# Down projections of the first MLP's chunks, taken in pairs as seven block products

## The chip, the cores and the metric

The kernel runs on one core of a Trainium2 chip. The metric is the device time in microseconds. It took 2169.54 us, the median of three runs (2168.88 to 2170.97).

## The reference, cut to what matters

Two layers. Each has attention, an MLP called cms, a second MLP called mod, a clip, and an adapter with a layer norm. Four batches of 512 tokens with 512 features; the hidden width of both MLPs is 2048, everything is float32.

```python
attn_out = softmax(q @ k.T * scale) @ v @ Wp + bp
cms_out  = gelu(attn_out @ cW1 + cb1) @ cW2 + cb2 + target_embed
modifier = gelu(concat([attn_out, cms_out]) @ mW1 + mb1) @ mW2 + mb2
x = clip(x + cms_out + modifier, 0, 1)       # then the adapter
```

The change touches only `gelu(...) @ cW2`, the down projection of cms.

## The kernel before

Two batches (b = 0, 1) are worked on together; two layers of two such groups give four rounds. Activations lie transposed, 128 features x 512 tokens a tile. Each float32 operand is split into a high part, written by ScalarE's `Copy` into float32r, and a low part, written by VectorE as value minus high part. A product is three matmuls a tile pair, hi*hi, hi*lo and lo*hi (`tile`, lines 610 to 619).

Both MLPs run over the hidden width in eight chunks of 256. A slot n (0 to 15 a round) computes the up projection of chunk n and the down projection of the chunk before it: slots 0 to 7 are cms, 8 to 15 mod. Up projections use Strassen-Winograd's scheme: the four block products over (feature half, batch) are replaced by seven, Q1 to Q7, of sums of blocks (A11, A12, S1, S2, A22, S3, S4 for the weights; B11, B21, T1, B22, T2, T3, T4 for the activations). GpSimd forms the weight sums (`sums`, line 542), and in mod the hidden sums (`hidden_sum`, line 557). In mod the down projection also has seven products, whose inner halves are the two 128-feature tiles of one chunk. In cms it is plain: `down(r, n, b)` (line 826) gives for each batch four banks of PSUM, two inner tiles each, 24 matmuls, 48 a chunk; `down_add` (line 1483) adds each bank to `pc`.

The order is written out by hand, an own program for each engine (`slot` for ScalarE at line 1180 and for VectorE at line 1570, `mlp` for TensorE at line 853), tied by counting semaphores. A chunk's weights go from memory to one of three staging buffers, are summed there, and are split into `ring`, in pieces: part 0 of A (four blocks, 1024 columns), part 1 (three blocks, 768 columns), D (a plain down piece, 1024 columns). `weight_stream` (line 148) lists the pieces; a load waits until the last piece of the buffer's former content is split (`STAGE_FREE`). The A pieces of cms chunks alternate between stages 0 and 1, D uses stage 2. Other names: `take` is ScalarE's copy of an up product out of bank 0 or 1 (`prod_done` is TensorE's signal, `snapped` its own); `combine` is VectorE's sum of an up product and that copy, into `raw`; `gelu` writes `raw`; `hidden_hi` and `hidden_lo` split it.

## Time and profile before

| | us |
|---|---|
| median of three runs | 2169.54 |
| profiled execution | 2169.18 |
| its span | 2167.5 |
| TensorE busy | 2107.3 (97%) |
| VectorE busy | 1548.4 (71%) |
| ScalarE busy | 1042.0 (48%) |
| GpSimd busy | 646.2 (30%) |

PE is TensorE's matmuls, PEld its weight loads, DVE VectorE, ACT ScalarE, POOL GpSimd, SPq the queue of SyncE, which issues the loads. The profiled execution's time is 1.68 us more than its span. The duration in a matmul's row is its length in the pipeline; the next one begins before it ends. Queries used: the page, busy time by stretch, instructions in order of time of each engine, groups by line and form, and the waits.

### The profile page before, as it was taken

Reading aid. Unit: us, or ns where it says so; the run is one execution under the profiler, and the core shown is the slowest. Engines: PE = TensorE matmul, PEld = TensorE weight load, DVE = VectorE, ACT = ScalarE, POOL = GpSimd, SP = SyncE. Lnnn points to the kernel's source line nnn. Section 1 sums busy time; section 2 is a strip of 40 time slices with the busy share of each in tenths; the row PEclk is TensorE's granted clock in tenths of the full one; section 3 lists DMA queues with packets and bytes.
Section 4 is the critical chain, followed back from the end, with each engine's and each line's share of the span. In section 5 each row is a group of like instructions: output and inputs, shape, how many; then the busy total and the mean of one; then the engine's idle time right before and its main releaser. Section 6 shows DMA issues by size and latency. Waiting matters only on the chain.

```text
span 2167.5 us, 24870 instructions
## 1 busy us (share of the span) xinstructions
PE 2107.3 (97%) x9256; PEld 1724.2 (80%) x9256; DVE 1548.4 (71%) x1923; ACT 1042.0 (48%) x1527; POOL 646.2 (30%) x644
## 2 busy tenths in 40 slices
PE   8999998999999998999999999899999999999997
PEld 6888886888878886888877888688887888778884
DVE  4366678776867668876776766977686865887776
ACT  5264445544446444544554544444454644354444
POOL 1001147453001116655000111854400011475420
PEclk9999999999999999999999999999999999999999
DMA  8101111112302111112312111121130311112111
...
DMA packets 124615, 138.02 MB, mean 64 GB/s; under 512 B 5824, under 2 KB 100032, under 8 KB 123600
## 3 DMA queue, kind: packets, MB, share of 16 engines
...
## 4 chain that ended last, share of the span: by engine, by line
PE 83%; DVE 11%; ACT 3%; issue 2%; DMA 2%; SPq 0%; ACTq 0%; DVEq 0%
PE bank L615 27%; PE bank L617 27%; PE bank L616 27%; DVE ring L1321 2%; DVE vc L1363 2%; DMA fold_staging<-fold_w 1%; DVE pc L1493 1%; ACT ring L955 1%; DVE lsum L1695 1%; DVE xa L1358 1%; ACT raw L1098 0%; PE bank L923 0%; DVE xs L1700 0%; DVE xs L1653 0%; DVE xs L1685 0%
## 5 line engine op out<-in xcount | busy, mean ns | idle before, releaser
L550 POOL TENSOR_TENSOR stage<-stage 128x256 f32<-128x256 f32 x120 | 112.6, 938 | 1120.4 <-DMA stage<-cms_w 903.5
L1321 DVE TENSOR_TENSOR ring<-stage,ring 128x1024 fp32r<-128x1024 f32 (+1 forms) x312 | 365.1, 1181 | 103.8 <-ACT ring L955 103.5
L615 PE MATMUL bank<-ph_hi,ring 128*128 128x512 f32 x1048 | 410.6, 392 | 5.3 <-issue 2.4
L617 PE MATMUL bank<-ph_hi,ring 128*128 128x512 f32 x1048 | 407.9, 389 | 0.0
L616 PE MATMUL bank<-ph_lo,ring 128*128 128x512 f32 x1048 | 407.9, 389 | 0.0
L615 PE MATMUL bank<-xa,ring 128*128 128x512 f32 x1016 | 396.2, 390 | 5.7 <-DVE ring L1321 2.8
L617 PE MATMUL bank<-xa,ring 128*128 128x512 f32 x1016 | 395.3, 389 | 0.0
L616 PE MATMUL bank<-xa,ring 128*128 128x512 f32 x1016 | 395.3, 389 | 0.0
L955 ACT ACTIVATE ring<-stage 128x1024 fp32r<-128x1024 f32 (+1 forms) x312 | 296.3, 970 | 111.3 <-PE bank L617 78.3
L615 PEld LDWEIGHTS bank<-ph_hi,ring 128*128 128x128 f32 x1048 | 196.7, 188 | 53.7 <-issue 7.2
L616 PEld LDWEIGHTS bank<-ph_lo,ring 128*128 128x128 f32 x1048 | 196.8, 188 | 40.8 <-issue 0.7
L617 PEld LDWEIGHTS bank<-ph_hi,ring 128*128 128x128 f32 x1048 | 196.7, 188 | 40.8
L615 PEld LDWEIGHTS bank<-xa,ring 128*128 128x128 f32 x1016 | 190.7, 188 | 48.4 <-DVE ring L1321 7.9
L1517 DVE TENSOR_TENSOR ph_lo<-raw,ph_hi 128x512 fp32r<-128x512 f32 x312 | 213.7, 707 | 17.4 <-ACT ph_hi L1103 17.3
L617 PEld LDWEIGHTS bank<-xa,ring 128*128 128x128 f32 x1016 | 190.7, 188 | 39.6
L616 PEld LDWEIGHTS bank<-xa,ring 128*128 128x128 f32 x1016 | 190.7, 188 | 39.6
L615 PE MATMUL bank<-vc,ring 128*128 128x512 f32 x512 | 201.0, 393 | 16.9 <-DVE vc L1363 10.7
L617 PE MATMUL bank<-vc,ring 128*128 128x512 f32 x512 | 199.4, 389 | 0.0
L616 PE MATMUL bank<-vc,ring 128*128 128x512 f32 x512 | 199.3, 389 | 0.0
L1493 DVE TENSOR_TENSOR pc<-bank,pc 128x512 f32<-128x512 f32 x224 | 152.2, 688 | 60.6 <-PE bank L617 60.3
L1103 ACT ACTIVATE ph_hi<-raw 128x512 fp32r<-128x512 f32 x144 | 88.0, 629 | 200.2 <-PE bank L617 198.5
L1504 DVE TENSOR_TENSOR raw<-bank,snap 128x512 f32<-128x512 f32 x112 | 77.1, 688 | 144.5 <-PE bank L617 140.3
...
## 6 DMA issues: line engine op xcount, KB each, us to landing
stage<-mod_w SPq DMA_DIRECT2D x128, 256.0 KB, 3.3
...
```

The source lines that it names most:

```text
L550: pool.tensor_tensor(part(S1), part(S2), part(A22), ALU.add).then_inc(sums_ready, 1)
L615: pe.matmul(dst, lh, rh, start=start and n == 0, stop=False, skip_group_check=not start)
L616: pe.matmul(dst, lh, rl, start=False, stop=False, skip_group_check=not start)
L617: done = pe.matmul(dst, ll, rh, start=False, stop=n == last, skip_group_check=not start)
L955: act.activation(ring_part(key, 0), staged(key), ACT.Copy).then_inc(w_hi, 1)
L1103: act.activation(ph_hi[:, tile, :], raw[:, tile, :], ACT.Copy).then_inc(h_hi, 1)
L1321: dve.tensor_tensor(ring_part(key, 1), staged(key), f32(ring_part(key, 0)), ALU.subtract).then_inc(w_lo, 1)
L1358: dve.tensor_tensor(xa[:, 8 + 4 * b + k:8 + 4 * b + k + 2, :], src[:, b, k:k + 2, :], f32(xa[:, 4 * b + k:4 * b + k + 2, :]), ALU.subtract ...
L1363: dve.tensor_tensor(block_lo(t, blk, j, n), src, f32(block_hi(t, blk, j, n)), ALU.subtract).then_inc(lo_sem, 1)
L1493: done = dve.tensor_tensor(acc, src, acc, ALU.add)
L1504: dve.tensor_tensor(raw[:, to, :], bank[BANK[q]][:, :], snap[:, 0, :], ALU.add).then_inc(combined, 1)
L1517: done = dve.tensor_tensor(ph_lo[:, at, :], src, f32(ph_hi[:, at, :]), ALU.subtract)
```

## The change

Chunks (0,1), (2,3) and (4,5) of cms form pairs i = 0, 1, 2. A pair's down projection is one product with an inner width of 512: its inner halves are the two chunks, its outer halves the two halves of the 512 features, its columns the two batches. It is computed as seven block products of 2 x 2 tile pairs, 12 matmuls each. Of pair i, Q1 and Q5 run in its odd slot 2i+1, Q3 and Q6 in the even slot after it, Q7, Q4 and Q2 in the odd slot after that. Chunks 6 and 7 stay plain, in slot 7. What comes with it:
- a piece E a pair, with blocks of 512 columns, in stages 1 and 2 together; it is loaded by four transfers, summed by four 512-wide GpSimd additions, and split in four parts (1024, 512, 1024, 1024 columns). All A pieces now use stage 0;
- GpSimd forms eight hidden sums a pair (T1, T3, T2, T4 for both tiles), and fourteen tiles a pair are split where eight were;
- a buffer `raw_odd` for the odd chunk's hidden tiles, and places in `vc` for high and low parts; both are free in cms;
- seven adds of 1024 columns a pair into `pc` where sixteen of 512 stood (the first ones with the bias stay 512 wide);
- up products start with Q5 in slots 2 to 7, Q3 comes ahead of Q7 in slots 1 to 6;
- slot 7: the remaining products of pair 2, then both plain down projections of chunk 6, then the rest; D of chunk 7 is split ahead of them.

```diff
+PAIR_AT = {A11: 0, S1: 1, A12: 2, A22: 3, S2: 4, S3: 5, S4: 6}
+PAIR_PARTS = ((0, 2), (6, 1), (2, 2), (4, 2))
+PAIR_RING_GROUP = (4, 11, 14, 4)
...
+def up_order(n):
+    return 0 if n == CH - 1 else 1 if n == SLOTS - 1 else 3 if 1 < n < CH else 2
...
     def staged_up(r, n):
-        pieces.append(((r, "A", n), n % 2 if n < CH else 0))
+        pieces.append(((r, "A", n), 0))
         if n >= CH:
...
+    def pair_first(r, n):
+        pieces.append(((r, "E", n), 1))
+        ops.append((r, "E", n, 0))
...
+            def load_pair(r, n):
+                sp.wait_ge(w_lo, STAGE_FREE[r, "E", n])
+                for c, blocks in ((n - 1, (PAIR_AT[A11], PAIR_AT[S4])), (n, (PAIR_AT[A12], PAIR_AT[A22]))):
+                    src = cms_w[2 * (r // 2 * CH + c) + 1, :, :].rearrange("p (k m n) -> p k m n", k=2, m=2)
+                    for m, to in enumerate(blocks):
+                        sp.dma_start(stage_pair[:, to, :].rearrange("p (k n) -> p k n", k=2), src[:, :, m, :]).then_inc(stage_in[1], 16)
...
+            def pair_sum(r, i, blk, j):
+                c = 2 * i
+                if blk == T1:
+                    pool.wait_ge(gelu_done, gelu_at(r, c, 2 + j))
+                    pool.wait_ge(h_lo, pair_split_at(r, i, B11, j))
+                    pool.tensor_tensor(raw[:, j, :], raw[:, j, :], raw[:, 2 + j, :], ALU.subtract).then_inc(hid_sum, 1)
+                elif blk == T3:
+                    pool.wait_ge(gelu_done, gelu_at(r, c + 1, 2 + j))
+                    pool.wait_ge(hid_sum, pair_sum_at(r, i, T1, j))
+                    pool.tensor_tensor(raw[:, 2 + j, :], raw_odd[:, 2 + j, :], raw[:, 2 + j, :], ALU.subtract).then_inc(hid_sum, 1)
+                elif blk == T2:
+                    pool.wait_ge(h_lo, pair_split_at(r, i, B22, j))
+                    pool.wait_ge(hid_sum, pair_sum_at(r, i, T3, j))
+                    pool.tensor_tensor(raw_odd[:, 2 + j, :], raw[:, j, :], raw_odd[:, 2 + j, :], ALU.add).then_inc(hid_sum, 1)
+                else:
+                    pool.wait_ge(h_lo, pair_split_at(r, i, B21, j))
+                    pool.wait_ge(hid_sum, pair_sum_at(r, i, T2, j))
+                    pool.tensor_tensor(raw_odd[:, j, :], raw_odd[:, 2 + j, :], raw_odd[:, j, :], ALU.subtract).then_inc(hid_sum, 1)
...
             for r in range(ROUNDS):
-                for n in range(1, CH + 1):
-                    sums((r, "A", n))
+                sums((r, "A", 1))
+                sums((r, "E", 1))
+                for n in range(1, CH):
+                    i = n // 2
+                    if n % 2 and paired(n):
+                        pair_sum(r, i, T1, 0)
+                        pair_sum(r, i, T1, 1)
+                        sums((r, "A", n + 1))
+                        for j in range(2):
+                            pair_sum(r, i, T3, j)
+                            pair_sum(r, i, T2, j)
+                    elif n % 2 == 0:
+                        pair_sum(r, i - 1, T4, 0)
+                        pair_sum(r, i - 1, T4, 1)
+                        sums((r, "A", n + 1))
+                        if paired(n):
+                            sums((r, "E", n + 1))
+                sums((r, "A", CH))
                 sums((r, "C", CH))
...
+            def pair_product(r, i, q):
+                blk, at = OPERAND[q], RING_E[q] * BLK
+                pe.wait_ge(w_lo, W_AT[r, "E", 2 * i + 1, PAIR_GROUP[q]])
+                pe.wait_ge(h_lo, pair_split_at(r, i, blk, 1))
+                before = {Q6: Q1, Q7: Q6, Q4: Q7, Q3: Q5, Q2: Q3}
+                if q in before:
+                    pe.wait_ge(added, pair_down_at(r, i, before[q]))
+                elif i:
+                    pe.wait_ge(added, pair_down_at(r, i - 1, Q4 if q == Q1 else Q2))
+                two = pair[int(q in (Q5, Q3, Q2))]
+                for j in range(2):
+                    tile(two[:, j, :], [(ring[:, 0, at + k * BLK + j * P:at + k * BLK + (j + 1) * P],
+                                         ring[:, 1, at + k * BLK + j * P:at + k * BLK + (j + 1) * P],
+                                         pair_hi(blk, k), pair_lo(blk, k)) for k in range(2)],
+                         down_done if j else None, start=q in (Q1, Q5, Q2))
+            def pair_even(r, n):
+                i = n // 2 - 1
+                up(r, n, Q5)
+                up(r, n, Q1)
+                pair_product(r, i, Q3)
+                up(r, n, Q6)
+                up(r, n, Q2)
+                up(r, n, Q3)
+                up(r, n, Q7)
+                pair_product(r, i, Q6)
+                up(r, n, Q4)
+            def pair_odd(r, n):
+                i = n // 2
+                for q in UP_ORDER[up_order(n)][:2]:
+                    up(r, n, q)
+                if i:
+                    pair_product(r, i - 1, Q7)
+                up(r, n, Q6)
+                up(r, n, Q2)
+                if i:
+                    pair_product(r, i - 1, Q4)
+                up(r, n, Q3)
+                if i:
+                    pair_product(r, i - 1, Q2)
+                up(r, n, Q7)
+                pair_product(r, i, Q1)
+                up(r, n, Q4)
+                pair_product(r, i, Q5)
...
+                i = n // 2 - 1
+                act.wait_ge(down_done, pair_down_at(r, i, Q5))
+                split_hi((r, "E", n - 1, 3))
+                split_hi((r, "A", n, 1))
                 take(r, n, Q1, bank[BANK[Q2]][:, :])
-                if not first:
-                    split_hi((r, "D", n - 1))
+                pair_t_hi(r, i, T3, 0)
+                pair_b_hi(r, i, B21, 1)
+                pair_t_hi(r, i, T2, 0)
                 take(r, n, Q5, snap[:, 0, :])
+                pair_t_hi(r, i, T3, 1)
+                pair_t_hi(r, i, T2, 1)
+                pair_t_hi(r, i, T4, 0)
                 take(r, n, Q6, bank[BANK[Q3]][:, :])
-                act.wait_ge(prod_done, prod_at(r, n, Q2))
-                act.wait_ge(h_lo, hidden_at(r, n - 1, 0))
-                gelu(r, n, 0, bank[BANK[Q2]][:, :])
...
+                i = n // 2
+                if i:
+                    split_hi((r, "A", n, 1))
+                split_hi((r, "E", n, 1))
+                if i == 0:
+                    split_hi((r, "E", n, 0))
+                    act.wait_ge(gelu_done, gelu_at(r, 0, 3))
+                take(r, n, Q1, bank[BANK[Q2]][:, :])
+                if i:
+                    pair_b_hi(r, i, B11, 1)
+                take(r, n, Q5, snap[:, 0, :])
+                pair_t_hi(r, i, T1, 0)
+                pair_t_hi(r, i, T1, 1)
+                if i:
+                    act.wait_ge(down_done, pair_down_at(r, i - 1, Q7))
+                    split_hi((r, "E", n, 0))
+                take(r, n, Q6, bank[BANK[Q3]][:, :])
+                up_turn(r, n, 0)
+                split_hi((r, "A", n + 1, 0))
+                up_turn(r, n, 2)
+                pair_b_hi(r, i, B22, 0)
+                if i:
+                    act.wait_ge(down_done, pair_down_at(r, i - 1, Q2))
+                pair_b_hi(r, i, B21, 0)
+                split_hi((r, "E", n, 2))
+                up_turn(r, n, 3)
+                pair_b_hi(r, i, B22, 1)
+                up_turn(r, n, 1)
...
+            def pair_add(r, i, q):
+                b, m = DRAIN[q]
+                acc, src = pc[:, b, m:m + 2, :], pair[int(q in (Q5, Q3, Q2))]
+                minus = q in (Q5, Q7, Q4)
+                dve.wait_ge(down_done, pair_down_at(r, i, q))
+                if q not in PAIR_FIRST_DRAIN:
...
+                if i == 0 and q in PAIR_FIRST_DRAIN:
+                    dve.wait_ge(attn_lo, (r + 1) * ATT_BUILDS)
+                    for j in range(2):
+                        done = dve.tensor_scalar(acc[:, j, :], src[:, j, :], -1.0 if minus else 1.0,
+                                                 cbias[:, 2 * r + b, m + j:m + j + 1], ALU.mult, ALU.add)
+                elif minus:
+                    done = dve.tensor_tensor(acc, acc, src[:, :, :], ALU.subtract)
+                else:
+                    done = dve.tensor_tensor(acc, src[:, :, :], acc, ALU.add)
+                done.then_inc(added, 1)
...
+                i = n // 2 - 1
+                pair_add(r, i, Q5)
+                split_lo((r, "E", n - 1, 3))
+                split_lo((r, "A", n, 1))
+                pair_split_lo(r, i, T3, 0)
+                pair_split_lo(r, i, B21, 1)
+                pair_split_lo(r, i, T2, 0)
+                pair_split_lo(r, i, T3, 1)
+                pair_add(r, i, Q3)
+                pair_split_lo(r, i, T2, 1)
+                combine(r, n, C12)
+                pair_split_lo(r, i, T4, 0)
+                combine(r, n, C22)
+                split_lo((r, "A", n + 1, 0))
+                pair_add(r, i, Q6)
+                pair_split_lo(r, i, T4, 1)
+                if paired(n):
+                    pair_split_lo(r, i + 1, B11, 0)
+                else:
+                    hidden_lo(r, n, 0)
+                    hidden_lo(r, n, 2)
+                    hidden_lo(r, n, 3)
...
+                i = n // 2
+                if i:
+                    split_lo((r, "A", n, 1))
+                split_lo((r, "E", n, 1))
+                if i:
+                    pair_split_lo(r, i, B11, 1)
+                    pair_add(r, i - 1, Q7)
+                pair_split_lo(r, i, T1, 0)
+                pair_split_lo(r, i, T1, 1)
+                split_lo((r, "E", n, 0))
+                split_lo((r, "A", n + 1, 0))
+                if i:
+                    pair_add(r, i - 1, Q4)
+                combine(r, n, C12)
+                combine(r, n, C22)
+                pair_split_lo(r, i, B22, 0)
+                if i:
+                    pair_add(r, i - 1, Q2)
+                pair_split_lo(r, i, B21, 0)
+                split_lo((r, "E", n, 2))
+                pair_add(r, i, Q1)
+                pair_split_lo(r, i, B22, 1)
```

VectorE, a slot of cms in the middle of round 0. Before (slot 4; `stage2` holds D, `stage1` or `stage0` A, L1493 is `down_add`, L1504 `combine`, L1517 a low part, L1321 a ring piece):

```order
L1321 TENSOR_TENSOR ring_62<-stage2_59,ring_62 128x1024
L1504 TENSOR_TENSOR raw_55<-bank0,snap_56 128x512
L1493 TENSOR_TENSOR pc_51<-bank45,pc_51 128x512
L1321 TENSOR_TENSOR ring_62<-stage1_58,ring_62 128x1024
L1493 TENSOR_TENSOR pc_51<-bank45,pc_51 128x512
L1493 TENSOR_TENSOR pc_51<-bank67,pc_51 128x512 x2
L1517 TENSOR_TENSOR ph_lo_53<-raw_55,ph_hi_52 128x512
L1504 TENSOR_TENSOR raw_55<-bank3,snap_56 128x512
L1517 TENSOR_TENSOR ph_lo_53<-raw_55,ph_hi_52 128x512
L1493 TENSOR_TENSOR pc_51<-bank45,pc_51 128x512
L1321 TENSOR_TENSOR ring_62<-stage1_58,ring_62 128x768
L1493 TENSOR_TENSOR pc_51<-bank45,pc_51 128x512
```

After, slot 4 (`stage_pair` holds E, `stage0` A; L1885 and L1887 are `pair_add`, L1793 `combine`, L1865 and L1862 low parts, L1613 a ring piece):

```order
L1885 TENSOR_TENSOR pc_52<-pc_52,bank67 128x1024
L1613 TENSOR_TENSOR ring_64<-stage_pair_61,ring_64 128x1024
L1613 TENSOR_TENSOR ring_64<-stage0_58,ring_64 128x768
L1865 TENSOR_TENSOR vc_50<-raw_56,vc_50 128x512
L1865 TENSOR_TENSOR vc_50<-raw_odd_51,vc_50 128x512
L1862 SCALAR_TENSOR_TENSOR vc_50<-raw_odd_51,vc_50 128x512
L1865 TENSOR_TENSOR vc_50<-raw_56,vc_50 128x512
L1887 TENSOR_TENSOR pc_52<-bank67,pc_52 128x1024
L1862 SCALAR_TENSOR_TENSOR vc_50<-raw_odd_51,vc_50 128x512
L1793 TENSOR_TENSOR raw_56<-bank3,snap_57 128x512
L1865 TENSOR_TENSOR vc_50<-raw_odd_51,vc_50 128x512
L1793 TENSOR_TENSOR raw_56<-bank0,snap_57 128x512
```

Plain adds were the filler between ring pieces; now low parts of hidden tiles and their sums follow each other from the slot's start, behind one wide add and two ring pieces.

ScalarE, the opening of a slot of cms. Before, slot 3 (L1103 a high part, L1091 `take`, L955 a ring piece, L1098 `gelu`):

```order
L1103 ACTIVATE ph_hi_52<-raw_55 128x512 x2
L1091 ACTIVATE bank2<-bank0 128x512
L955 ACTIVATE ring_62<-stage2_59 128x1024
L1091 ACTIVATE snap_56<-bank1 128x512
L1091 ACTIVATE bank3<-bank0 128x512
L1098 ACTIVATE raw_55<-bank2,vec_66 128x512
L955 ACTIVATE ring_62<-stage1_58 128x1024
L1098 ACTIVATE raw_55<-raw_55,vec_66 128x512
```

After, slot 3 (L1169 ring pieces, L1305 `take`, L1396 and L1400 high parts, L1312 `gelu`):

```order
L1169 ACTIVATE ring_64<-stage0_58 128x768
L1169 ACTIVATE ring_64<-stage_pair_61 128x512
L1305 ACTIVATE bank2<-bank0 128x512
L1396 ACTIVATE ph_hi_53<-raw_56 128x512
L1305 ACTIVATE snap_57<-bank1 128x512
L1400 ACTIVATE ph_hi_53<-raw_56 128x512 x2
L1169 ACTIVATE ring_64<-stage_pair_61 128x1024
L1305 ACTIVATE bank3<-bank0 128x512
L1312 ACTIVATE raw_odd_51<-bank2,vec_68 128x512
```

The copies out of banks 0 and 1 now stand behind a ring piece of A and the 512-wide part of E, and three high parts and a ring piece lie between them.

GpSimd, from slot 1 on. Before, with nothing but the weight sums of the next chunks:

```order
L550 TENSOR_TENSOR stage0_57<-stage0_57 128x256
L551 TENSOR_TENSOR stage0_57<-stage0_57 128x256
L553 TENSOR_TENSOR stage0_57<-stage0_57 128x256
L555 TENSOR_TENSOR stage0_57<-stage0_57 128x256
L550 TENSOR_TENSOR stage1_58<-stage1_58 128x256
L551 TENSOR_TENSOR stage1_58<-stage1_58 128x256
```

After, from the middle of slot 2 (L711 T4's sums, L667 to L672 the weight sums of A, then of E, L699 the T1 sums of the next pair; the sums T3 and T2, L703 and L707, stand ahead of these rows):

```order
L711 TENSOR_TENSOR raw_odd_51<-raw_odd_51 128x512 x2
L667 TENSOR_TENSOR stage0_58<-stage0_58 128x256
L668 TENSOR_TENSOR stage0_58<-stage0_58 128x256
L670 TENSOR_TENSOR stage0_58<-stage0_58 128x256
L672 TENSOR_TENSOR stage0_58<-stage0_58 128x256
L667 TENSOR_TENSOR stage_pair_61<-stage_pair_61 128x512
L668 TENSOR_TENSOR stage_pair_61<-stage_pair_61 128x512
L670 TENSOR_TENSOR stage_pair_61<-stage_pair_61 128x512
L672 TENSOR_TENSOR stage_pair_61<-stage_pair_61 128x512
L699 TENSOR_TENSOR raw_56<-raw_56 128x512 x2
```

A's sums now wait behind hidden sums, and E's follow A's.

## Rows read from the trace of the kernel before

**Rows 1.** The page: busy us by engine, and the ended-last chain's shares.

```profile
PE 2107.3 (97%) x9256; PEld 1724.2 (80%) x9256; DVE 1548.4 (71%) x1923; ACT 1042.0 (48%) x1527; POOL 646.2 (30%) x644
...
PE 83%; DVE 11%; ACT 3%; issue 2%; DMA 2%; SPq 0%; ACTq 0%; DVEq 0%
```

**Rows 2.** Busy us by stretch (PE, PEld, DVE, ACT, POOL), clock, DMA: cms, then mod.

```profile
700.00:806.00 106.00, 106.00 (x470) 87.76 (x469) 65.52 (x89) 50.96 (x75) 17.21 (x22) 1.00 0.18 55
870.00:1060.00 190.00, 189.38 (x836) 156.56 (x835) 141.20 (x154) 91.75 (x134) 94.38 (x98) 1.00 0.19 58
```

**Rows 3.** In order of time (start, length): TensorE, cms slots of round 1.

```profile
715.28 0.39 PE L615 MATMUL bank<-ph_hi,ring 128*128 128x512 f32 x1
...
735.68 0.39 PE L615 MATMUL bank<-ph_hi,ring 128*128 128x512 f32 x1
```

**Rows 4.** In order of time: VectorE, the same slots.

```profile
715.54 0.69 DVE L1504 TENSOR_TENSOR raw<-bank,snap 128x512 f32<-128x512 f32 x1 [1.42 <-PE bank L617]
716.15 0.68 DVE L1517 TENSOR_TENSOR ph_lo<-raw,ph_hi 128x512 fp32r<-128x512 f32 x1
...
729.69 1.22 DVE L1321 TENSOR_TENSOR ring<-stage,ring 128x1024 fp32r<-128x1024 f32 x1
730.83 0.69 DVE L1493 TENSOR_TENSOR pc<-bank,pc 128x512 f32<-128x512 f32 x1
```

**Rows 5.** In order of time: ScalarE, the same slots.

```profile
722.28 0.58 ACT L1091 ACTIVATE bank<-bank 128x512 f32<-128x512 f32 x1 [0.21 <-PE bank L617]
722.78 1.05 ACT L955 ACTIVATE ring<-stage 128x1024 fp32r<-128x1024 f32 x1
723.73 0.59 ACT L1091 ACTIVATE snap<-bank 128x512 f32<-128x512 f32 x1
```

**Rows 6.** In order of time: SyncE's queue, the load of an A piece.

```profile
705.10 1.22 SPq L442 DMA_DIRECT2D stage<-cms_w  x2
```

**Rows 7.** In order of time: GpSimd, sums of that piece; hidden sums in mod.

```profile
710.06 1.05 POOL L550 TENSOR_TENSOR stage<-stage 128x256 f32<-128x256 f32 x1 [15.53 <-DMA stage<-cms_w]
...
712.71 0.75 POOL L555 TENSOR_TENSOR stage<-stage 128x256 f32<-128x256 f32 x1
...
885.79 1.30 POOL L562 TENSOR_TENSOR raw<-raw 128x512 f32<-128x512 f32 x1
887.23 2.10 POOL L566 TENSOR_TENSOR raw<-raw 128x512 f32<-128x512 f32 x1
```

**Rows 8.** Slot 8 in order of time; then groups, 700 to 806 and 870 to 1060.

```profile
829.12 6.04 POOL L585 TENSOR_TENSOR xs<-xs,pc 128x512 f32<-128x512 f32 x4 [20.18 <-DVE pc L1493]
...
831.89 4.34 DVE L1363 TENSOR_TENSOR vc<-pc,vc 128x1024 fp32r<-128x1024 f32 x2 [1.13 <-ACT vc L981]
...
L1517 DVE TENSOR_TENSOR ph_lo<-raw,ph_hi 128x512 fp32r<-128x512 f32 x22 | 14.8, 694 | 0.0
L1321 DVE TENSOR_TENSOR ring<-stage,ring 128x1024 fp32r<-128x1024 f32 x11 | 13.5, 1224 | 5.9 <-ACT ring L955 5.9
...
L1321 DVE TENSOR_TENSOR ring<-stage,ring 128x1024 fp32r<-128x1024 f32 x22 | 29.2, 1329 | 0.5 <-ACT ring L955 0.5
L1517 DVE TENSOR_TENSOR ph_lo<-raw,ph_hi 128x512 fp32r<-128x512 f32 x41 | 28.3, 715 | 0.0
```

**Rows 9.** In order of time: ScalarE, the opening of slot 1.

```profile
681.75 0.59 ACT L1091 ACTIVATE bank<-bank 128x512 f32<-128x512 f32 x1
...
684.21 0.58 ACT L1091 ACTIVATE bank<-bank 128x512 f32<-128x512 f32 x1 [0.40 <-PE bank L617]
```

**Rows 10.** TensorE's waits, 600 to 660 (attention): us, times, longest.

```profile
PE bank L615 <- DVE vc L1330: 1.3, 1, 1.3
PE bank L654 <- DVE pc L1340: 1.0, 1, 1.0
```

**Rows 11.** TensorE's waits, 806 to 870 (slots 7 and 8).

```profile
PE bank L615 <- DVE ring L1321: 2.7, 4, 1.5
PE bank L615 <- DVE vc L1363: 2.7, 2, 1.7
```

347 lines of the change are left out of this document (242 added, 105 removed).

## The prediction, made before the changed kernel ran

> **What bounds the kernel now.** I read the page first: its row of busy times and the shares of the chain that ended last [rows 1]. TensorE is busy for 97% of the span and makes up 83% of the chain. Then the table of stretches. In 106 us of cms chunks TensorE has not one idle microsecond, while VectorE is at 62%, ScalarE at 48% and GpSimd at 16% [rows 2]. So in these slots only fewer matmuls can help, and only a new wait can hurt. Then TensorE's list in order of time: the first matmul of a chunk's second down half starts at 715.28, that of the next chunk at 735.68 [rows 3]. Between them lie one slot's 90 matmuls (42 of the up projection, 48 of the down projection), so one matmul costs 20.40/90 = 0.2267 us. The 389 ns of a matmul's own row is its length in the pipeline, and it overlaps the next. Reckoning with 389 would make this change look worth 56 us.
>
> **What goes.** A plain down projection of two chunks costs 2 x 48 = 96 matmuls. The pair costs seven products of 2 x 2 x 3 = 12, that is 84. Three pairs in each of four rounds: 12 x 12 = 144 fewer, and the order of TensorE's rows falls by exactly 144. 144 x 0.2267 = 32.6 us.
>
> **The new slots.** An up product has 6 matmuls (1.36 us), a pair product 12 (2.72). An even slot has seven up and two pair products, 14.96 us; an odd one from the second pair on has five pair products, 23.12; the first odd slot has two, 14.96. Before, each took 20.40. Below, times count from the start of the slot. Other engines start 0.26 us after TensorE goes on to its next product (715.28 against 715.54) [rows 3, 4].
>
> VectorE: an operation of 512 columns occupies 0.61, of 1024 1.14 [rows 4], of 768 I take 0.87, between them. An even slot holds three adds of 1024 from PSUM, ring pieces of 1024, 768 and 1024, two combines and eight low parts: 3.42 + 3.15 + 1.22 + 4.88 = 12.7 of 14.96 us. The odd one holds 4.56 + 4.9 + 1.22 + 3.66 = 14.3 of 23.12. A pair is thus 27.0 of 38.1 us. That is hidden, but the even slot is 85% full, where before it was 62%. ScalarE: high parts at 0.50 to 0.52, 1024 columns at 0.95 [rows 5]; it is never full.
>
> The tight chain of an even slot. All A pieces now use stage 0, so the next chunk's load waits until VectorE has split the second part of this chunk's A:
> - VectorE adds Q5's product from 0.26 to 1.40, splits E's part 3 to 2.54 and A's part 1 to 3.4.
> - Two transfers, from the first issue to GpSimd's first sum: 705.10 to 710.06, 4.96 us [rows 6, 7]; GpSimd starts at about 8.5.
> - Three of four sums: 710.06 to 712.71, 2.65 [rows 7], so 11.15. ScalarE's high part to 12.1, VectorE's low part to 13.3.
> - TensorE wants it at 14.96. Slack 1.6 us.
>
> Behind those sums GpSimd adds the next pair's E blocks, which are 512 wide. No row shows that form on the stage; its nearest is a hidden sum of 512, 1.44 from start to start [rows 7]. It lies between 0.88 (a 256-wide sum) and 2.1 (the longest such row). I take 1.44, the row of the same width: 8.5 + 3.5 + 5.8 = 17.8. In the next slot ScalarE has E's part 1 ahead of the copy of Q1, done at 18.9; TensorE needs that copy at 14.96 + 5.44 = 20.4. Slack 1.5, or minus 1.2 at 2.1 a sum. Queued behind this piece on ScalarE are the copies of Q1, Q5 and Q6, on which TensorE waits. The copy of Q6 in an even slot stands after eight ScalarE operations that follow Q1's end: 2.98 + 9 x 0.52 = 7.7, against 8.16.
>
> So the slacks are small and collisions between VectorE and GpSimd decide how much of them is left. The trace shows the collisions: two low parts of 1024 with both inputs in SBUF take 4.34 us beside GpSimd's four residual adds, 2.2 each and not 1.22 [rows 8]. It also shows them in a milder mix. In 190 us of mod chunks, GpSimd 50% busy [rows 2], a ring piece is 1329 ns and not 1224, a low part 715 and not 694 [rows 8]: 22 x 0.105 + 41 x 0.021 = 3.2 us, 0.034 per us of GpSimd. A pair gives GpSimd 12 sums of 512 and 8 of 256, about 12 x 1.35 + 8 x 0.8 = 22.6 us, hence 0.8 us; doubled for the denser VectorE, 1.5 us a pair. This is below either slack, but not by much.
>
> The Trainium skill (SBUF — State Buffer, "Who interferes with whom") says that a VectorE instruction with two SBUF inputs and a GpSimd instruction that reads SBUF exclude each other for the whole instruction. The rows agree where both engines run dense: 2.2 for 1.22. By that rule applied to every GpSimd sum the pair would not fit; that is the second rival, and the mod chunks are the row against it.
>
> **The other edits.**
> - First odd slot: ahead of the copy of Q1, ScalarE had two high parts (1.04) and now has E's parts 1 and 0 (0.50 + 0.95), 0.4 later. The copy started at 681.75 and ends 0.5 later; Q6's end (the copy at 684.21 less 0.26) puts the start of Q6 at 682.59 [rows 9]. 0.34 of room, so 0.1 lost: 4 x 0.1 = 0.4. At most the whole 0.4 each: 1.6.
> - Attention: GpSimd's four E sums of the first pair now fall there. TensorE waits 2.3 us there in round 1 for VectorE [rows 10], so this is on the path. Between 0 (VectorE reads PSUM mostly) and 1.1 a round (one 512 sum in the way). I take 0.5, nearer the first: 3 rounds, 1.5.
> - Last cms slot: D of chunk 7 is split earlier. TensorE waits 2.7 us on ring pieces and 2.7 on the operands of the cms output there [rows 11]. The second stays. Of the first I take a gain of 0.25 a round, 1.0, between 0 and 2.7 x 4 = 10.8, near the lower end, as most of these waits stand behind the cms output.
> - Even slots, 12 of them: slack 1.6 against collisions that come in steps of up to 0.95. I take 0.3 each, 3.6. Ends: 0 and 1.6 (a sum in the way at three of the four VectorE steps, less the slack, and a bit of a late load), 19.
> - Odd slots after an E sum, 8: 0.3 each, 2.4. Ends: 0 and 1.2, 9.6.
> - More load descriptors, one more wait per product: their work lies under TensorE's products. Nothing, or a few tenths.
>
> **Sum.** The profiled execution took 2169.18 us (span 2167.5 and 1.68 around it), 0.36 under the median shown. 2169.18 - 32.6 + 0.4 + 1.5 - 1.0 + 3.6 + 2.4 = 2143.5; by the median, 2143.9. I forecast 2144.
>
> **Rivals.**
> 1. The single stage for A. If loads land later (E's megabyte is issued right behind it) or GpSimd reaches A's sums late, each even slot ends on its last VectorE step. For: it is a chain of five steps over four engines in the shortest slot, where before A alternated between two stages. Against: 1.6 us of slack by the rows. Losing 2.9 in the chain leaves 1.3 a slot: 12 x 1.3 = 16, less the 3.6 already counted, 2156.
> 2. Slower: the shared access to SBUF. If every sum holds up a VectorE operation as beside the residual adds, 12 x 0.95 + 8 x 0.5 = 15.4 us come on top of 27.0, and VectorE needs 42.4 us for a pair against 40.8 before: 12 x 1.6 = 19 slower, 2189. It decides from 40.8 - 27.0 = 13.8 us of collisions a pair, and costs part of the gain from 11.1 on. For: the two-times rows [rows 8]. Against: VectorE's adds and combines read PSUM, and the mod chunks show a twentieth of that.
> 3. Nothing waits: 2169.5 - 32.6 - 1 = 2136. For: 1.5 us of slack at each place and a granted clock of 1.00 [rows 2]. Against: three places with under 0.5.
>
> **How the numbers follow.** The forecast, 2138 to 2150, has 0.55; rival 1 (2150 to 2162) 0.22; rival 3 (2135 to 2138) 0.10; rival 2 0.09; the rest, a mixture that ends between 2162 and the old time, 0.04. The range 2135.5 to 2160 leaves out a part of rival 1 and all of rival 2. A change under 0.2% (4.3 us) can't be told from none: faster 0.89, same 0.03, slower 0.08.
>
> **What would show it.** TensorE: 9112 matmuls for 9256, and slots of 15.0, 15.0, 23.1, 15.0, 23.1, 15.0 us. Right if its idle time grows by under 3 us a round. The A chain shows as TensorE waiting for a ring piece at the first up product of slots 3, 5 and 7; E's sums as ScalarE waiting for GpSimd at the start of slots 3 and 5; collisions as a mean of VectorE's low parts well above 0.75 us. I am wrong if VectorE is the longest part of the chain in the cms slots, or if an even slot takes over 16.5 us.

## The result and the profile after

The changed kernel takes 2178.79 us (median of 5 runs, 2175.84 to 2180.72) against 2169.54: 1.0044 times the time before, interval 1.003 to 1.0058. It is slower by 0.4%, where 1.2% faster was forecast. The profiled execution's span is 2177.0 us.

The page, busy times and chain (against [rows 1]):

```profile
PE 2095.5 (96%) x9112; PEld 1697.2 (78%) x9112; DVE 1689.8 (78%) x1927; ACT 1094.2 (50%) x1623; POOL 895.3 (41%) x788
...
PE 67%; DVE 20%; ACT 4%; issue 4%; DMA 2%; POOL 2%; SPq 1%; ACTq 0%; DVEq 0%; POOLq 0%
```

The 144 matmuls are gone. VectorE has only 4 instructions more than before, yet is busy 141 us longer. Its share of the chain rises from 11% to 20%; in the cms slots 1 to 7 of round 1 it is 59 us of the chain and TensorE 42, where it was 7 and 140. Slots 1 to 4 of round 1 without their first 0.8 us, as a stretch (columns as in [rows 2]):

```profile
684.30:756.70 72.40, 69.65 (x298) 54.76 (x296) 64.16 (x63) 45.41 (x72) 49.74 (x38) 1.00 0.17 51
```

TensorE is idle for 2.75 of 72.4 us, where it had no idle at all. VectorE is at 89%, GpSimd at 69% (it was at 62% and 16%). The starts of slots in TensorE's timeline (against [rows 3]):

```profile
715.35 0.50 PE L768 MATMUL bank<-xa,ring 128*128 128x512 f32 x1 [0.66 <-DVE ring L1613]
...
739.44 0.39 PE L768 MATMUL bank<-xa,ring 128*128 128x512 f32 x1
...
756.72 0.50 PE L768 MATMUL bank<-xa,ring 128*128 128x512 f32 x1 [1.36 <-DVE ring L1613]
```

Slot 3 took 24.09 us and slot 4 17.28; at 0.2267 a matmul they need 23.12 and 14.96. Adding up each stage from the first matmul of one to that of the next, over four rounds:

| Stage | forecast, us | measured |
|---|---|---|
| 144 matmuls | -32.6 | -32.6 |
| slot 1 | +0.4 | +1.2 |
| even slots (12) | +3.6 | +17.5 |
| odd slots from the second pair (8) | +2.4 | +10.4 |
| last cms slot (4) | -1.0 | +2.6 |
| attention | +1.5 | +10.5 |
| everything else | 0 | -0.1 |
| sum | -25.7 | +9.5 |

So the cms slots gave back 31.7 of the 32.6 us, and attention made it a loss. The mod chunks, slot 8 and the rest are as before to a few tenths.

**How it comes about, in one slot.** VectorE in slot 4 of round 1 (739.44 to 756.72) and just before it, in order of time (against [rows 4]):

```profile
737.21 2.31 DVE L1613 TENSOR_TENSOR ring<-stage_pair,ring 128x1024 fp32r<-128x1024 f32 x1
...
741.17 1.21 DVE L1885 TENSOR_TENSOR pc<-pc,bank 128x1024 f32<-128x1024 f32 x1
742.30 1.40 DVE L1613 TENSOR_TENSOR ring<-stage_pair,ring 128x1024 fp32r<-128x1024 f32 x1
743.62 2.05 DVE L1613 TENSOR_TENSOR ring<-stage,ring 128x768 fp32r<-128x768 f32 x1
...
747.40 1.78 DVE L1865 TENSOR_TENSOR vc<-raw,vc 128x512 fp32r<-128x512 f32 x1
749.10 1.21 DVE L1887 TENSOR_TENSOR pc<-bank,pc 128x1024 f32<-128x1024 f32 x1
750.24 0.67 DVE L1862 SCALAR_TENSOR_TENSOR vc<-raw_odd,vc 128x512 fp32r<-128x512 f32 x1
...
754.65 2.02 DVE L1613 TENSOR_TENSOR ring<-stage,ring 128x1024 fp32r<-128x1024 f32 x1 [1.94 <-ACT ring L1169]
756.59 1.21 DVE L1887 TENSOR_TENSOR pc<-bank,pc 128x1024 f32<-128x1024 f32 x1
```

GpSimd in the same time (against [rows 7]), with the load of the next A piece:

```profile
742.58 2.28 POOL L711 TENSOR_TENSOR raw_odd<-raw_odd 128x512 f32<-128x512 f32 x1
746.96 1.67 POOL L711 TENSOR_TENSOR raw_odd<-raw_odd 128x512 f32<-128x512 f32 x1 [2.10 <-DVE vc L1865]
750.59 0.92 POOL L667 TENSOR_TENSOR stage<-stage 128x256 f32<-128x256 f32 x1 [1.96 <-DMA stage<-cms_w]
...
754.30 1.28 POOL L667 TENSOR_TENSOR stage_pair<-stage_pair 128x512 f32<-128x512 f32 x1
755.55 2.27 POOL L668 TENSOR_TENSOR stage_pair<-stage_pair 128x512 f32<-128x512 f32 x1
...
745.70 1.21 SPq L547 DMA_DIRECT2D stage<-cms_w  x2
```

Read ends, not starts. VectorE's low part starts at 747.40 and should be done at 748.08. GpSimd's sum ends at 746.96 + 1.67 = 748.63, and the low part at 749.18, which is 0.55 later: nearly all of its own work, done after the sum. The ring piece at 754.65 ends at 756.67, 1.09 after the sum of 754.30 has ended at 755.58. It goes the other way round too: the sum that starts at 755.55 ends at 757.82, 1.15 after VectorE's piece. That ring piece is the one for which TensorE opens slot 5 late, at 756.72. VectorE's adds from PSUM (1.21) are not touched.

The same can be counted over the whole trace: every VectorE addition or subtraction with both inputs in SBUF that starts while a GpSimd sum has over 0.13 us to run. There are 206 such meetings, listed singly, in the whole execution, and 194 of the operations are over 0.15 us longer than alone. In all 206 the end lies within 0.02 us of the same place: 0.55 us after the end of the sum for 512 columns, 0.82 for 768 and 1.08 for 1024. That is the operation's own time (0.68, 0.95, 1.22) less 0.13. The operations that read PSUM, 197 meetings of the same kind, are longer by 0.002 us on average. So but for those 0.13 us the two engines exclude each other, instruction by instruction.

The Trainium skill (SBUF — State Buffer, "Who interferes with whom") says that a VectorE instruction with two SBUF inputs contends with a GpSimd instruction that reads SBUF, and of the pair of ports they share: "Whoever issues first gets the shared pair for the whole instruction". The trace agrees, but for the 0.13 us.

Groups of the whole execution (busy, mean ns of one, idle before). Alone, 1024 columns take 1.22 us and 512 take 0.68:

```profile
L1613 DVE TENSOR_TENSOR ring<-stage_pair,ring 128x1024 fp32r<-128x1024 f32 x36 | 64.6, 1796 | 0.0
L1865 DVE TENSOR_TENSOR ph_lo<-raw,ph_hi 128x512 fp32r<-128x512 f32 x48 | 48.6, 1019 | 5.3 <-ACT ph_hi L1400 4.8
L1865 DVE TENSOR_TENSOR vc<-raw,vc 128x512 fp32r<-128x512 f32 x24 | 29.4, 1227 | 0.0
...
L711 POOL TENSOR_TENSOR raw_odd<-raw_odd 128x512 f32<-128x512 f32 x24 | 47.5, 1979 | 25.2 <-DVE vc L1865 25.2
```

Over the cms slots 1 to 7, these operations of VectorE take 107.7 us longer than alone, against 10.8 before: 9.0 us a pair.

**How it reaches TensorE.** In slot 4 VectorE starts late: the ring piece at 737.21 was held 1.09 us in slot 3, and the add of Q5's product starts 1.73 us into the slot, where 0.26 was reckoned. That is 1.5 us. The two ring pieces behind it add 1.3 (1.10 of it at 743.62), GpSimd's first three sums 0.3, and the piece at 754.65 another 0.8. Together 3.9 us, less 1.6 of slack: the slot is 2.3 us late. GpSimd's own queue isn't the cause here. It stood idle for 1.96 us until the load landed, and the load was issued at 745.70, when VectorE's held piece was done at 745.67. It is so in all twelve even slots: GpSimd waits 1.1 to 2.2 us for the load, and A's sums begin 10.2 to 11.3 us into the slot, where 8.5 was reckoned.

Only 7.6 of the even slots' 17.5 us stand at the opening of the next slot (slot 3 in four rounds, slot 5 in two, slot 7 in one). The rest stands inside: 4.4 at pair Q3, which waits for the late add of Q5's product, and 5.5 at pair Q6, which waits for the low parts of T2. In slot 4 the last of these is the one at 750.24, late by the hold at 747.40:

```profile
751.01 0.47 PE L768 MATMUL bank<-vc,ring 128*128 128x512 f32 x1
```

Of the odd slots' 10.4 us, 5.9 stand at up Q6, which waits for ScalarE's copy behind GpSimd's E sums, and 2.5 at pair Q4, behind an add of VectorE.

**Attention.** VectorE, GpSimd and TensorE in round 1:

```profile
642.17 4.88 DVE L2070 TENSOR_SCALAR xs<-xs,avec 128x512 f32<-128x512 f32 x4
...
641.18 1.30 POOL L667 TENSOR_TENSOR stage_pair<-stage_pair 128x512 f32<-128x512 f32 x1 [1.31 <-DMA stage_pair<-cms_w]
642.43 1.48 POOL L668 TENSOR_TENSOR stage_pair<-stage_pair 128x512 f32<-128x512 f32 x1
643.98 1.35 POOL L670 TENSOR_TENSOR stage_pair<-stage_pair 128x512 f32<-128x512 f32 x1
645.41 1.36 POOL L672 TENSOR_TENSOR stage_pair<-stage_pair 128x512 f32<-128x512 f32 x1
...
653.12 3.31 PE L807 MATMUL bank<-ident,pc 128*128 128x128 f32 x16 [4.04 <-DVE pc L1632]
```

Four tensor_scalar operations, which have one SBUF tensor as input, take 4.88 us beside the E sums. Before, the same four took 1.82 at this place:

```profile
643.00 1.82 DVE L1706 TENSOR_SCALAR xs<-xs,avec 128x512 f32<-128x512 f32 x4
```

TensorE then waits 4.04 us for what stands behind them on VectorE, against 1.0 in [rows 10].

Waits in the whole execution, of TensorE and then of ScalarE (us, times, longest). Of the 15.7 us some 10 stand at the start of mod, as in the kernel before, which has 10.9 in all:

```profile
PE bank L768 <- DVE ring L1613: 15.7, 19, 1.5
...
PE bank L807 <- DVE pc L1632: 10.3, 3, 4.0
...
PE bank L768 <- ACT bank L1305: 3.8, 2, 1.9
```

```profile
ACT ring L1169 <- POOL stage L670: 84.5, 48, 3.4
...
ACT ring L1169 <- POOL stage_pair L672: 32.6, 8, 4.8
```

### The profile page after: what moved, and what is told of

It is laid out like the page before. It is cut to its first block, busy times and chain, and to the rows that moved or that the text cites. A ratio compares the mean times of both kernels' runs of the same rounds, so it can differ in the third digit from the quotient of the medians.

```text
span 2177.0 us, 24902 instructions
## 1 busy us (share of the span) xinstructions
PE 2095.5 (96%) x9112; PEld 1697.2 (78%) x9112; DVE 1689.8 (78%) x1927; ACT 1094.2 (50%) x1623; POOL 895.3 (41%) x788
## 4 chain that ended last, share of the span: by engine, by line
PE 67%; DVE 20%; ACT 4%; issue 4%; DMA 2%; POOL 2%; SPq 1%; ACTq 0%; DVEq 0%; POOLq 0%
PE bank L768 22%; PE bank L770 22%; PE bank L769 22%; DVE ring L1613 6%; DVE vc L1655 2%; DMA stage<-cms_w 2%; DVE ph_lo L1865 2%; ACT ring L1169 1%; DVE pc L1887 1%; DVE pc L1780 1%; ACT raw L1312 1%; DVE lsum L2059 1%; DVE pc L1885 1%; DVE xa L1650 1%; DVE pc L1882 1%
## 5 line engine op out<-in xcount | busy, mean ns | idle before, releaser
L1613 DVE TENSOR_TENSOR ring<-stage,ring 128x1024 fp32r<-128x1024 f32 (+1 forms) x288 | 377.2, 1321 | 111.5 <-ACT ring L1169 111.1
L768 PE MATMUL bank<-xa,ring 128*128 128x512 f32 x1016 | 398.8, 393 | 15.8 <-DVE ring L1613 8.5
L667 POOL TENSOR_TENSOR stage<-stage 128x256 f32<-128x256 f32 x120 | 110.0, 916 | 634.7 <-DMA stage<-cms_w 474.8
L1169 ACT ACTIVATE ring<-stage 128x1024 fp32r<-128x1024 f32 (+1 forms) x288 | 271.2, 963 | 158.8 <-POOL stage L670 84.5
L768 PE MATMUL bank<-ph_hi,ring 128*128 128x512 f32 x808 | 318.6, 394 | 7.2 <-issue 2.4
L770 PE MATMUL bank<-ph_hi,ring 128*128 128x512 f32 x808 | 314.7, 389 | 0.0
L769 PE MATMUL bank<-ph_lo,ring 128*128 128x512 f32 x808 | 314.6, 389 | 0.0
L768 PE MATMUL bank<-vc,ring 128*128 128x512 f32 x704 | 277.4, 394 | 20.5 <-DVE vc L1655 10.7
L770 PE MATMUL bank<-vc,ring 128*128 128x512 f32 x704 | 274.2, 390 | 0.0
L769 PE MATMUL bank<-vc,ring 128*128 128x512 f32 x704 | 274.2, 389 | 0.0
L768 PEld LDWEIGHTS bank<-ph_hi,ring 128*128 128x128 f32 x808 | 151.6, 188 | 50.7 <-issue 14.6
L768 PEld LDWEIGHTS bank<-vc,ring 128*128 128x128 f32 x704 | 132.1, 188 | 61.1 <-DVE vc L1655 15.9
L770 PEld LDWEIGHTS bank<-ph_hi,ring 128*128 128x128 f32 x808 | 151.6, 188 | 32.1
L769 PEld LDWEIGHTS bank<-ph_lo,ring 128*128 128x128 f32 x808 | 151.7, 188 | 31.1 <-issue 0.7
L1806 DVE TENSOR_TENSOR ph_lo<-raw,ph_hi 128x512 fp32r<-128x512 f32 x216 | 148.0, 709 | 16.0 <-ACT ph_hi L1317 16.0
L1772 DVE TENSOR_TENSOR xs<-bank,xs 128x1024 f32<-128x1024 f32 x104 | 126.7, 1218 | 42.5 <-PE bank L770 42.2
L770 PEld LDWEIGHTS bank<-vc,ring 128*128 128x128 f32 x704 | 132.1, 188 | 28.1
```

What stands on the lines that cost most here:

```text
L667: pool.tensor_tensor(part(S1), a21, part(A22), ALU.add).then_inc(sums_ready, 1)
L768: pe.matmul(dst, lh, rh, start=start and n == 0, stop=False, skip_group_check=not start)
L769: pe.matmul(dst, lh, rl, start=False, stop=False, skip_group_check=not start)
L770: done = pe.matmul(dst, ll, rh, start=False, stop=n == last, skip_group_check=not start)
L1169: act.activation(ring_part(key, 0), staged(key), ACT.Copy).then_inc(w_hi, 1)
L1613: dve.tensor_tensor(ring_part(key, 1), staged(key), f32(ring_part(key, 0)), ALU.subtract).then_inc(w_lo, 1)
```

## The experiments

Theory 1: GpSimd's new sums hold VectorE up, and what queues behind them is late. Theory 2: the single stage of the A pieces and VectorE's own volume are the bound. For each kernel the table gives the time, its ratio to the kernel before, TensorE's waits in cms slots 1 to 7, and what VectorE's operations with SBUF inputs took there beyond their time alone (all four rounds, from the timelines). Before, these two are 3.8 and 10.8 us.

| Kernel | us | ratio (interval) | waits | VectorE held |
|---|---|---|---|---|
| changed kernel | 2178.8 | 1.0044 (1.003 to 1.0058) | 33.1 | 107.7 |
| `early` | 2169.4 | 0.9995 (0.9985 to 1.0004) | 35.6 | 111.5 |
| `tinyE` | 2145.6 | 0.9884 (0.9868 to 0.9901) | 14.6 | 80.9 |
| `tinyT` | 2148.8 | 0.9899 (0.9882 to 0.9916) | 5.0 | 43.7 |
| `tinyET` | 2136.7 | 0.9844 (0.9828 to 0.9861) | 5.0 | 29.7 |
| `all3` | 2162.7 | 0.9967 (0.9958 to 0.9977) | 28.8 | 115.6 |
| `narrow_early` | 2163.9 | 0.9971 (0.9961 to 0.998) | 32.4 | 81.0 |
| `all4` | 2157.7 | 0.9947 (0.9931 to 0.9964) | 22.5 | 85.7 |
| `edve` | 2157.1 | 0.9944 (0.9928 to 0.9961) | 23.5 | 95.6 |
| `edve_order` | 2155.1 | 0.9938 (0.9921 to 0.9954) | 21.3 | 98.2 |
| `edve_all` | 2145.1 | 0.9891 (0.9874 to 0.9907) | 12.1 | 81.8 |
| `edve_q` | 2170.9 | 1.0005 (0.9996 to 1.0015) | 36.2 | 63.5 |

### Which sums cost it

`early` moves one load and two groups of sums:

```diff
+                load_pair(r, 1)
                 load((r, "P"), cms_w[2 * (r // 2) * CH, :, :])
                 load_up(r, 1)
-                load_pair(r, 1)
...
-                sums((r, "A", 1))
+                if r:
+                    pool.wait_ge(rstd_ready, (r - 1) * GROUP + 1)
                 sums((r, "E", 1))
+                sums((r, "A", 1))
```

> The first pair's E piece of each round is loaded ahead of P and A, and its four GpSimd sums run when VectorE has finished the first reciprocal of the layer norm (where it is idle for 7.4 us in the attention), not when it multiplies by gamma. Nothing else moves. Theory 1 (GpSimd's sums hold up VectorE's fp32 tensor_scalar, 4.88 us where 1.82 stood, and TensorE's transposes wait for it): the attention goes back to its old length in rounds 1 to 3, 10.4 us less, about 2168.5 us, no different from the kernel before. Theory 2 (the attention is late for another reason, such as the order of loads): no change, 2179 us.

`tinyE` makes the four E weight sums 8 columns wide, `tinyT` the eight hidden sums of a pair; both leave the rest of those sums out. `tinyE` fills the blocks by three more transfers (not shown in the cut). `tinyET` does both.

```diff
-                    return s[:, at[block], :]
+                    return s[:, at[block], 0:wide]      # tinyE: wide = 8 for E
...
-    pool.tensor_tensor(raw[:, j, :], raw[:, j, :], raw[:, 2 + j, :], ALU.subtract).then_inc(hid_sum, 1)
+    pool.tensor_tensor(raw[:, j, 0:8], raw[:, j, 0:8], raw[:, 2 + j, 0:8], ALU.subtract).then_inc(hid_sum, 1)
```

> Leaves out E's weight sums: GpSimd adds 8 of 512 columns, the other blocks are filled by three more transfers. The hidden sums stay. Theory 1 (collisions of GpSimd's sums with VectorE, and the queue on GpSimd): the attention's 10.4 us and the 5.8 us of waits for the copy of Q1 in slots 3 and 5 go, and some 4 to 6 us of late VectorE steps: about 2157 us. Theory 2 (the cms slots are late because VectorE and ScalarE have more splits to do and A has one stage, whatever GpSimd does): only the attention comes back, 2168 us.

> Leaves out the pair's hidden sums: GpSimd adds 8 of 512 columns, in the same order with the same waits. E's sums stay. Theory 1: eight sums a pair no longer hold up VectorE's ring pieces and low parts, and A's sums start earlier; of 31.7 us of waits in the cms slots about 12 go: 2167 us. The attention is unchanged. Theory 2: under 3 us, 2177 us.

> Leaves out both (E's weight sums and the pair's hidden sums, 8 of 512 columns each). All of TensorE's, VectorE's and ScalarE's work is as in the changed kernel. Theory 1: what is left of the waits is slot 7's 4 us and 2 to 4 us of the short chain, so the 32.6 us of matmuls show in full: 2139 to 2145 us, close to the forecast. Theory 2: 2160 us or more, since VectorE's 27 us a pair and the chain over one stage are still there.

`early` takes the whole attention loss away: rounds 1 to 3 take 95.6 us each there and not 99.2 to 100.1, and the slots wait 2.5 us more. `tinyE`, which keeps the order of the loads, has 95.6, 96.2 and 95.6 there, so it is the sums and not the loads. In `early` the four operations are back to their time alone:

```profile
645.10 1.82 DVE L2072 TENSOR_SCALAR xs<-xs,avec 128x512 f32<-128x512 f32 x4
```

`tinyET` ends at 2136.7 with the single A stage and all loads in place. In it every even slot takes 14.96 us and slots 3 and 5 take 23.12, exactly their matmuls. That refutes theory 2. It also shows that the chain with 1.6 us of slack was reckoned rightly, for a VectorE that nobody holds: its even slots end their last ring piece at 13.0 to 14.0 us, where 13.3 was reckoned; in the changed kernel it is 15.7 to 17.3. In `tinyT` the E sums are whole, and each of slots 2 to 6 is within 0.01 us of its matmuls: without the hidden sums no loss is left there. The ring piece of E and the low part of `tinyT`, as groups:

```profile
L1613 DVE TENSOR_TENSOR ring<-stage_pair,ring 128x1024 fp32r<-128x1024 f32 x36 | 43.9, 1219 | 0.7 <-ACT ring L1169 0.7
...
L1865 DVE TENSOR_TENSOR vc<-raw,vc 128x512 fp32r<-128x512 f32 x24 | 16.6, 692 | 8.8 <-ACT vc L1400 7.0
```

They are back from 1796 to 1219 and from 1227 to 692. What `tinyT` keeps is the attention loss (95.6, 96.1, 96.6 before; here 100.0, 100.5, 98.9), and that is its distance to `tinyET`. Each of the two gains more than theory 1 expected, by 11 and 18 us, and `tinyET` 2 more than its lower end. The losses of the two kinds of sums don't add up: of the 28.1 us of waits in the slots that go with both, 18.5 go without the E sums alone and all 28.1 without the hidden sums alone. That both fall on chains with little slack would explain it; no run shows it. These kernels also take work from GpSimd. For the even slots its idle time ahead of A's sums rules its own queue out. At up Q6 of the odd slots GpSimd's E sums are part of the chain, and there the runs don't part the hold from GpSimd's own time.

### Order and width

`all3` is `early` with the splits in another order (even slots: A part 1 ahead of E part 3; odd slots: the E parts behind the copy of Q5):

```diff
+                split_hi((r, "A", n, 1))
                 act.wait_ge(down_done, pair_down_at(r, i, Q5))
                 split_hi((r, "E", n - 1, 3))
-                split_hi((r, "A", n, 1))
...
-                split_hi((r, "E", n, 1))
                 take(r, n, Q1, bank[BANK[Q2]][:, :])
...
                 take(r, n, Q5, snap[:, 0, :])
+                if i:
+                    split_hi((r, "E", n, 1))
```

> The order of the writing inside the slots, on top of the E piece loaded first: in the even slots ScalarE and VectorE split the A weight sum before the last third of the E piece, in the odd slots the E weight sums are split after the copy of Q5, in slot 1 the E blocks after the copy of Q6. Theory 1a (the waits of TensorE come from what stands in front of the late piece: ScalarE is held by GpSimd's E sums ahead of its copy, and the chain of the one A stage starts behind the E piece): the wait at up Q6 of slots 1, 3 and 5 (3.2 us in four rounds) goes, and half of that at up Q5 (12.2 us): 2160 us, 2157 to 2164. Theory 1b (VectorE is late by the volume of its held-up work, whatever the order): the same waits turn up at another product of the slot, 2167 to 2171 us. A late copy or sum behind the reordered splits could also make it slower, up to 2175.

The waits of which 1a spoke, at up Q5 and up Q6, went altogether (15.3 us). But 6.7 us came up at pair Q6 and 1.4 at pair Q3, and VectorE is held as long as ever. 1a gives the time, and 1b is half right on the mechanism.

`narrow_early` is `early` with halves, of the hidden sums (one of four cases shown) and of E's weight sums:

```diff
-                    pool.tensor_tensor(raw[:, j, :], raw[:, j, :], raw[:, 2 + j, :], ALU.subtract).then_inc(hid_sum, 1)
+                    pool.tensor_tensor(raw[:, j, 0:BLK], raw[:, j, 0:BLK], raw[:, 2 + j, 0:BLK], ALU.subtract)
+                    pool.tensor_tensor(raw[:, j, BLK:2 * BLK], raw[:, j, BLK:2 * BLK], raw[:, 2 + j, BLK:2 * BLK], ALU.subtract).then_inc(hid_sum, 1)
```

> With the E piece loaded first, each 512-wide sum that GpSimd makes for a pair (E weights, hidden activations) is written as two of 256 elements; the same elements are read and written. If VectorE's instruction is held until the GpSimd instruction beside it has ended, it loses at most half as much each time: VectorE's held-up time in the cms slots falls from some 108 us towards 55 to 75, and the time to 2155 to 2164 us. If the two engines merely share the bandwidth of the buffer, the elements count and nothing changes but GpSimd's instruction starts (24 to 48 more for each round, some 0.1 us each): 2168 to 2173 us. If each start of a GpSimd instruction costs VectorE a wait of its own, it is slower: 2173 to 2182.

`all4` is both:

> The two edits before it together, all sums still on GpSimd: the reordered splits, and each 512-wide pair sum as two of 256. In the run with the halved sums alone 17.6 of 32.4 us of TensorE's waits in the cms slots stood at up Q6 of slots 3 and 5, the copy that ScalarE makes behind the E weight sums; in the run with the order alone, 18.5 of 28.8 us stood at pair Q3 and Q6, behind VectorE's held-up low parts. Theory 1 (two separate losses: the queue behind the late sums, and the hold of VectorE): each edit takes the other's remainder, 2144 to 2154 us, most likely 2149. If the two edits merely move one loss about, the time stays at that of either, 2160 to 2166 us.

The same elements in instructions of half the length held VectorE 30 us less, so the hold goes by instruction. At 81.0 it stayed above the 55 to 75 that I expected. The gain of 5.5 us is at the small end, since two halves together take longer than one whole and GpSimd's sums end later. TensorE's wait for ScalarE's copies behind the E sums, 3.8 us in the changed kernel and not listed in `early`, is 14.7 in `narrow_early`, and `all4` keeps 11.0:

```profile
PE bank L780 <- ACT bank L1317: 14.7, 8, 1.9
```

```profile
PE bank L780 <- ACT bank L1317: 11.0, 8, 1.8
```

`all4` missed its interval by 4 us: the late E splits only moved the queue on ScalarE from up Q6 to up Q3, where 12.9 of its 22.5 us of waits stand.

### The E sums on VectorE itself

`edve` has `early`, the odd-slot order of `all3`, and the E weight sums in VectorE's list:

```diff
+            def pair_weights(r, i):
+                ...
+                dve.tensor_tensor(part(S1), part(S4), part(A22), ALU.add).then_inc(e_sum, 1)
+                dve.tensor_tensor(part(S3), part(S4), part(A11), ALU.add).then_inc(e_sum, 1)
+                ...
-                            sums((r, "E", n + 1))
```

`edve_order` adds the even-slot order, `edve_all` also the halved hidden sums, `edve_q` quarters in place of halves.

> The four E weight sums of a pair are made by VectorE itself (0.68 us each) and not by GpSimd, with the E piece loaded first and the E blocks split behind the copy that TensorE waits for. Theory 1: what remains of GpSimd's work beside VectorE is the hidden sums and the A weight sums, as in the run without E sums, whose cms slots lost 14.6 us; VectorE has 2.7 us more a pair, of which some 1 us may show in each: 2146 to 2156 us, most likely 2150. Theory 2 (VectorE's own volume and the single A stage bound the pairs): 12 times 2.7 us more for VectorE turn up in the time, 2170 to 2185 us.

> The fastest version so far with the hidden sums again as 512-wide instructions: what the halves alone are worth once no copy waits behind them. If VectorE is held to the end of a GpSimd instruction, the wide ones cost more: 2148 to 2155 us against 2145.1. If only the number of elements counts, 2143 to 2147 us.

> As the run before it, and in the even slots the A sum split before the last third of the E piece, and GpSimd's hidden sums written as pairs of 256-wide ones. Theory 1: nearly all the waits in the cms slots go, as in the run with no pair sums on GpSimd (2136.7 us), but for VectorE's extra work: 2140 to 2148 us, most likely 2144. Theory 2: 2165 to 2180 us.

> The fastest version so far with each hidden sum of a pair as four instructions of 128 elements where it had two of 256. If VectorE is held to the end of the instruction beside it, its waits at pair Q6 and Q3 (8.1 us in four rounds) shrink further: 2139 to 2144 us. If each GpSimd instruction brings VectorE a wait of its own whatever its length, or if GpSimd's starts make the chain of the four sums longer than the slot gives it, 2146 to 2156 us.

48 more instructions on the engine that already made up 20% of the chain, and the time falls by 12 us from `early` to `edve`: theory 2 expected 2170 to 2185. Part of the 12 is the order of the odd slots, which `early` doesn't have. The pair that differs by the place of the E sums alone is `all3` and `edve_order`: 2162.7 to 2155.1, 7.6 us. `edve` ends 1 us above theory 1's interval. `edve_all` is 1.1% faster than the kernel before and 1.5% faster than the changed one, the best version here. Its chain again looks like [rows 1]:

```profile
PE 81%; DVE 13%; issue 3%; ACT 3%; DMA 0%; SPq 0%; ACTq 0%; DVEq 0%
```

Halving the hidden sums is worth 10 us between `edve_order` and `edve_all`. Quartering them loses 26 against the halves. Both halves of my expectation for `edve_q` came true at once: VectorE is held less, 63.5 us and not 81.8, but GpSimd's chain grew more. Groups of GpSimd in `edve_q`, the four quarters of one sum:

```profile
L718 POOL TENSOR_TENSOR raw_odd<-raw_odd 128x128 f32<-128x128 f32 x24 | 21.6, 900 | 0.0
L719 POOL TENSOR_TENSOR raw_odd<-raw_odd 128x128 f32<-128x128 f32 x24 | 18.1, 752 | 0.0
L720 POOL TENSOR_TENSOR raw_odd<-raw_odd 128x128 f32<-128x128 f32 x24 | 15.5, 646 | 0.0
L721 POOL TENSOR_TENSOR raw_odd<-raw_odd 128x128 f32<-128x128 f32 x24 | 21.7, 903 | 0.0
```

and ScalarE's wait for the last of them (15.9 us for the last half in `edve_all`), and TensorE's for ScalarE's copies behind it (not listed in `edve_all`):

```profile
ACT vc L1409 <- POOL raw_odd L721: 40.6, 24, 2.7
```

```profile
PE bank L775 <- ACT bank L1314: 22.7, 17, 2.5
```

One sum is now 3.2 us against 1.85 whole in `edve_order`, as each piece can meet a VectorE operation again: where it meets none, a sum of 512 columns takes 1.30 us, one of 256 0.74 and one of 128 0.46, so that four quarters alone would be 1.8. At 2170.9 it lies outside both intervals; the slower one was 2146 to 2156.

## Why the prediction was wrong

**Right.** The matmul's price and the 32.6 us: with nothing held, `tinyET` is 2136.7, and rival 3 said 2136. The five steps of the A chain and their slack, with VectorE free (`tinyET`). Some of the places: slots 3, 5 and 7 open on TensorE waiting for a ring piece (7.6 us, not in every round), ScalarE waits for GpSimd's E sums at the start of odd slots, the low parts of `raw` are over 0.75 us, and the marks of being wrong are there (six of twelve even slots over 16.5 us, the rest 15.8 to 16.4; VectorE the longest part of the chain in cms slots 1 to 7, with 51 to 59 us a round against TensorE's 42 to 45). Pair Q3, pair Q6 and pair Q4, where TensorE waits for VectorE inside the slots (12.3 us), were on no list of mine.

**The step that failed** is the size of the collisions: "0.034 per us of GpSimd", hence "1.5 us a pair". It measured 9.0. I took the average excess over all VectorE rows of the mod chunks as a property of the hardware. It was the product of a hard rule and of how rarely the two met there. In that stretch, of 42 such operations listed singly, 14 started beside a GpSimd sum with over 0.13 us to run, with a mean hold of 0.32 us. In the cms slots 1 to 6 of round 1 it was 2 of 32, and with the change it is 32 of 54, at 0.73 us. The evidence was in my own rows: the hidden sum of 2.10 us [rows 7] against 1.30 for its neighbour. It starts at 887.23, while this operation of VectorE runs, which itself started beside the sum of 885.79:

```profile
886.13 2.03 DVE L1321 TENSOR_TENSOR ring<-stage,ring 128x1024 fp32r<-128x1024 f32 x1 [0.47 <-ACT ring L955]
```

The first sum ends at 887.09, VectorE's piece at 888.16, 1.07 later, and the second sum at 889.33, 1.17 later. That is the whole rule in three rows of the kernel before. I weighed a rule of the skill against a mean and let the mean win. The mean can't speak against it.

**Even and odd slots, 6.0 forecast, 27.9 measured.** The slack of 1.6 us was set against one hold in a chain with five steps. There are three ring pieces of VectorE in it, a meeting costs 0.73 on average, and GpSimd's sums in the same chain are held in turn. The chain was also started at 0.26 us, as if VectorE came free; in slot 4 of round 1 it came 1.5 late from slot 3, and the two holds at 743.62 and 754.65, 2.05 - 0.95 = 1.10 and 2.02 - 1.22 = 0.80, were added to that. The upper ends that I gave were of the right size (19 for 17.5, 9.6 for 10.4), but the range of the time did not use them.

**Attention, 1.5 forecast, 10.5 measured.** I called VectorE's work there "mostly PSUM" and set an upper end of one sum a round. The four tensor_scalar operations read SBUF and lost 3.1 us in a row in round 1. `early`, and `tinyE` with the loads in place, show it to be all of the loss. **Last slot,** -1.0 forecast, 2.6 measured: I read the 2.7 us of waits for ring pieces [rows 11] as slots 7 and 8, but slot 9 begins at 858.17 in that window, and all but 0.2 us stand in it. There was next to nothing to gain. The waits at the two halves of chunk 7's down projection stayed as long as they were (3.9 us in four rounds before, 4.0 after), the first now for a low part and no longer for D, and one at up Q1 came (2.2). **Slot 1,** 0.4 forecast, 1.2 measured: up Q6 starts 0.3 us late in each round and not 0.1.

**Rival 2** had the mechanism and the wrong price on both sides. It said that holds cost something from 11.1 us a pair, by comparing VectorE's sum with TensorE's. The hold was 9.0, less than that, and cost 2.6 us a pair all the same. A hold at the end of a chain costs at once, whatever the engine's average load.

Open: how the 5.0 us that remain in `tinyET` in slots 1 and 7 could go, and why `edve_all` still loses 6.2 us at pair Q6; neither was tried.
